# Last addition of every second tile of the final combination by GpSimd between its gathers

## What is computed

```python
topk_w, topk_idx = jax.lax.top_k(scores, K)                 # K = 2
cw = jnp.zeros((T, E), jnp.float32).at[jnp.arange(T)[:, None], topk_idx].add(topk_w)
y = jnp.einsum('te,teh->th', cw, expert_out).reshape(b, s, h)
y = y + _swiglu_mlp(x, sw_gate, sw_up, sw_down).reshape(b, s, h)
...
x = x + gb * y
```

## Time and profile before

| | us |
|---|---|
| median of 3 runs | 1524.89 (1524.53 to 1525.71) |
| the profiled execution, in all | 1526.7 |
| its span, first to last instruction | 1524.5 |
| TensorE busy in it | 1502.2 (99%) |
| VectorE busy | 983.0 (64%) |
| ScalarE busy | 729.5 (48%) |
| GpSimd busy | 713.5 (47%) |

### The profile page before, as it was taken

One profiled execution on the slowest core, in us unless ns is written; L12 is line 12 of the kernel. 1 busy time (PEld: TensorE's weight loads), 2 busy tenths in 40 slices (PEclk: granted clock), 3 DMA queues, 4 the chain that ended last, 5 costly groups with the idle time before them and its releaser, 6 DMA issues.

```text
span 1524.5 us, 29262 instructions
## 1 busy us (share of the span) xinstructions
PE 1502.2 (99%) x8812; PEld 1340.2 (88%) x8812; DVE 983.0 (64%) x2213; ACT 729.5 (48%) x1733; POOL 713.5 (47%) x767
## 2 busy tenths in 40 slices
PE   8999999999999999999999999999999999999997
PEld 4788888887999999999999999988999899999986
DVE  5977666677777777777777777785458322222258
ACT  4532222346666666666666666663332233333323
POOL 1113333446766665666565665769822211111054
PEclk9999999999999999999999999999999999999999
DMA  9336555577858486666757485746543555765576
GB/s 321 125 139 228 193 194 193 210 265 239 252 171 247 141 255 184 202 182 208 216 164 231 145 244 165 234 161 225 196 163 140 199 201 190 282 233 194 195 230 226
DMA packets 205600, 311.92 MB, mean 205 GB/s; under 512 B 80641, under 2 KB 142465, under 8 KB 198609
## 3 DMA queue, kind: packets, MB, share of 16 engines
q1 hardware_dynamic: 198400, 287.04, 56.6%
q0 software_dynamic: 5680, 18.62, 4.1%
q10 hardware_dynamic: 1440, 5.24, 0.9%
HBM read 189.97 MB, written 120.88 MB: 204 GB/s over the span
## 4 chain that ended last, share of the span: by engine, by line
PE 85%; DMA 4%; POOL 4%; DVE 3%; issue 2%; ACT 1%; SPq 1%; POOLq 0%; another core or an unknown queue 0%; ACTq 0%; DVEq 0%
PE bank L1624 45%; PE bank L1738 17%; PE bank L1853 7%; PE bank L1805 7%; PE bank L1836 4%; PE bank L1907 2%; PE bank L1941 1%; DMA h<-slot_results,pos_i 1%; DMA mod_early<-wmod 1%; POOL acc L1071 1%; POOL acc L1069 1%; DMA keys<-k_ring 1%; DMA ffn_rows<-h 1%; DMA w<-experts_lo 0%; DMA xr<-x 0%
## 5 line engine op out<-in xcount | busy, mean ns | idle before, releaser
L1624 PE MATMUL bank<-w,xt 128*128 (+2 forms) x1608 | 287.5, 327 | 0.3 <-ACT gate_s L1552 0.2
L1624 PEld LDWEIGHTS bank<-w,xt 128*128 128x128 f32 x1608 | 261.9, 188 | 6.6 <-DVE xt L2271 0.6
L1448 ACT ACTIVATE prob<-prob,row_inv 128x128 f32<-128x128 f32 (+3 forms) x256 | 137.3, 560 | 78.5 <-DVE row_inv L2308 78.3
L2427 DVE TENSOR_TENSOR ht_lo<-bank,ht_hi 128x128 fp32r<-128x128 f32 (+1 forms) x213 | 48.4, 282 | 181.0 <-ACT ht_hi L1567 176.4
L1436 ACT ACTIVATE prob<-bank,neg_max 128x128 f32<-128x128 f32 (+3 forms) x256 | 133.8, 526 | 42.3 <-DVE neg_max L2300 42.1
L1624 PE MATMUL bank<-wv_hi,h_hi 128*128 128x256 f32 x512 | 147.1, 287 | 0.0
L1624 PE MATMUL bank<-w,ht_hi 128*128 (+3 forms) x426 | 138.7, 406 | 6.8 <-DVE ht_lo L2427 5.9
L1624 PE MATMUL bank<-wv_hi,h_lo 128*128 128x256 f32 x512 | 144.7, 283 | 0.0
L1624 PE MATMUL bank<-wv_lo,h_hi 128*128 128x256 f32 x512 | 144.7, 283 | 0.0
L1248 POOL DMA_INDIRECT xin<-ffn_rows,slot_tokens x39 | 39.8, 1019 | 185.1 <-PE bank L1907 181.4
L2295 DVE TENSOR_REDUCE row_max<-bank 128x1 f32<-128x128 f32 (+3 forms) x256 | 119.7, 488 | 6.6
(11 more groups left out here) (252 smaller groups left out, 3882.7 us busy)
## 6 DMA issues: line engine op xcount, KB each, us to landing
keys<-k_ring SPq DMA_DIRECT2D x64, 512.0 KB, 3.2
ch_raw<-wexp SPq DMA_DIRECT2D x128, 170.0 KB, 3.2
experts_hi<-ch_hi SPq DMA_DIRECT2D x128, 170.0 KB, 2.6
experts_lo<-ch_lo SPq DMA_DIRECT2D x128, 170.0 KB, 2.8
w<-experts_hi SPq DMA_DIRECT2D x9, 2176.0 KB, 7.8
w<-experts_lo SPq DMA_DIRECT2D x9, 2176.0 KB, 14.5
q_transposed<-q_out SPq DMA_DIRECT2D x64, 256.0 KB, 2.1
k_even<-keys SPq DMA_DIRECT2D x16, 1024.0 KB, 5.7
```

The costliest lines, as they stand in the source:

```text
L1448: ins = act.activation(part, part, ACT.Copy, scale=row_inv[:, h, r:r + 1])
L1624: ins = pe.matmul(dst, a, m, start=(k == 0), stop=(k == last))
```

## The change

For the odd places below 12 (i = 1, 3, 5, 7, 9, 11, which are tiles 0 to 5) VectorE stops after the multiplication and raises `f_ok` there. The addition into `acc` is done by GpSimd, in `add_tile(i - 4)`, placed directly ahead of the gathers for place i = 5, 7, 9, 11, 13, 15. The new addition raises `h2_ok`, whose count stood at 16 (NT) until then, and both GpSimd's gathers for that place and SyncE's store of the tile wait for that count in place of `f_ok`.

```diff
         def finished(i):
 
+            if i % 2 and i < 2 * NB1:
+                return h2_ok, NT + (i + 1) // 2
             return f_ok, i + 1
...
+            def add_tile(i):
+
+                row = acc[:, GATHER[i], :]
+                pool.wait_ge(f_ok, i + 1)
+                pool.tensor_tensor(row, row, h2[:, i % TT, :], ALU.add).then_inc(h2_ok, 1)
+
             for i, t in enumerate(GATHER):
                 if i >= TT:
+                    if (i - TT) % 2:
+                        add_tile(i - TT)
                     pool.wait_ge(*finished(i - TT))
...
-                link(dve.tensor_tensor(a, a, mods[:, t // TT, 3, :], ALU.mult))
+                ins = dve.tensor_tensor(a, a, mods[:, t // TT, 3, :], ALU.mult)
+                if i % 2 and i < 2 * NB1:
+                    ins.then_inc(f_ok, 1)
+                    return
+                link(ins)
                 dve.tensor_tensor(acc[:, t, :], acc[:, t, :], a, ALU.add).then_inc(f_ok, 1)
```

## The result

The changed kernel takes 1535.2 us (median of 5 runs, 1532.0 to 1537.1), the kernel before 1525.2 us beside it (5 runs, 1524.5 to 1526.5). The ratio of the two is 1.006 with a 95% interval of 1.0049 to 1.0071: **slower by 9.2 us**, where 6.2 was forecast. The direction and the mechanism hold; the size is 3 us short. 1.006 of the 1524.89 from which the forecast started is 1534.0, near the top of its range (1534.8); the median itself, 1535.2, lies 0.4 us past it.

A forecast was written before the change was run, and what follows sets the result against it. GpSimd's own queue was taken to bound the tail: last gather 7.2 us later, less 0.95 for a quicker landing, makes +6.2 us on 1524.9, forecast 1531.1 us, range 1526.8 to 1534.8.

The forecast's parts named there:

- The bound and its end: In the last 66 us, the span's end moves as the last gather (place 15) moves, unless something else becomes later.
- The walk over GpSimd's list: GpSimd's steps summed from place 4 on: six odd places of 4.97 us, five even of 2.62; last gather 7.2 us later.
- The addition: Each of the six additions on GpSimd was taken at 1.29 us, from 22 earlier ones of the same shape.
- The gap: On GpSimd, from an addition's end to the gather waiting for it: 0.80 us, lower bound 0.15.
- Rival 1: GpSimd's queue runs ahead: gather 0.15 us behind the addition, only the last addition shows, 1525.3 us; chance 0.11.
- The hold-up of an addition by VectorE: VectorE operations with two SBUF inputs hold off each GpSimd addition in the tail by 0.3 us, bounds 0 to 0.6.
- The hold-up of gathers: Gathers xr behind an addition were taken at 1.25 us, between 1.01 when queued and 1.48 after a wait.
- The waits for `f_ok`: GpSimd's waits for VectorE before even places would already be met, for place 14 with some 4 us to spare.
- The landing: The last gather, with emptier DMA engines, lands in 4.5 us instead of 5.45, giving back 0.95 (bounds 0 and 2.05).
- From landing to end nothing is changed: The closing chain behind the last gather's landing, VectorE's work and the last store, stays at 10.3 us.
- rival 3: Late loads, or additions meeting two VectorE operations, make TensorE wait in the last job: another 3 us, 1534; chance 0.12.
- rival 2: GpSimd's 6.9 us of waits hide the additions and VectorE's saving comes through: 1.4 us faster, 1523.5; chance 0.05.

The follow-up runs named there:

- e_double: The changed kernel with a second GpSimd addition of the same size ahead of each of the six; 1541.99 us, ratio 1.0109 to the kernel before.
- e_noadd: The changed kernel without GpSimd's six additions, which VectorE does not do either; 1524.54 us, ratio 0.9997 to the kernel before.
- a_again: The changed kernel, unedited, profiled a second time; 1534.61 us, ratio 1.0058 to the kernel before.
- a_third: The changed kernel, unedited, profiled a third time; a single execution, 1536.06 us.
- e_tiny: The changed kernel with each of GpSimd's six additions over 4 of 512 columns only, all waits kept; 1527.67 us, ratio 1.0018 to the kernel before.
- e_hwait: The changed kernel with the wait for the addition moved from gather xr to gather h; 1530.64 us, ratio 1.003 to the kernel before.
- b_again: The kernel before, unedited, profiled a second time; 1524.83 us, ratio 0.9994.
- e_last: The changed kernel with only place 11's addition on GpSimd, VectorE doing the others as before; 1527.09 us, ratio 1.0008 to the kernel before.
- e_half: The changed kernel with only the additions of places 1, 5 and 9 on GpSimd, the others on VectorE; 1527.34 us, ratio 1.0015 to the kernel before.

## Why the prediction was right, and where it was short

**The bound and its end: right.** "The end moves as the last gather moves, unless something else becomes later still." e_double shows the first half (7.5 us in, 7.4 to 7.8 out by the medians), e_noadd that nothing else of the change matters, and the second half is what the sum then left out.

**The walk over GpSimd's list: right in sum, its terms partly by luck.** It put the last gather 1515.95 - 1467.10 = 48.85 us behind the mark; it stands at 48.4, 50.6 and 50.4. Term by term:
- The addition, 1.29 taken, is 1.30. The gap, 0.80 taken, is 0.79 to 0.80 in all six places of after, a_again, a_third, e_double and e_tiny. Rival 1, that the queue runs ahead (0.15), holds only where another gather stands between (e_hwait).
- The hold-up of an addition by VectorE, 0.3 each, 1.8 in all: none. The six additions take 1.29 to 1.31 in the three traces. An addition starts right behind a gather, 0.02 us after its end, and where the two meet it is VectorE that is held.
- The hold-up of gathers, taken as 0.24 for the six xr only, 1.4 in all: up to the last gather's start it is 2.7 us in the first trace of after and 4.8 in a_again, and gathers h and even places are long too. -1.8 + 1.3 gives 48.35 for the 48.4, -1.8 + 3.4 gives 50.45 for the 50.6. The total came close to the first trace because one term was too high and another too low: that is luck.
- The waits for `f_ok` are met from place 5 on, as forecast.

**The landing: right.** 4.5 us taken; 3.6 (1518.47 to 1522.11 in after), 4.8 and 4.2 measured.'s 3.3 was not reached. The Trainium skill's figure for such a DMA (DMA: Bandwidth & Descriptors, "Anatomy of one DMA"), 2.6 us by its formula, was reached nowhere; the rows decide.

**"From landing to end nothing is changed": wrong, 1.3 us.** From landing to end it was 10.3 us in both b_again and the first trace; it is 11.3, 11.6 and 11.9 in the three traces of after. VectorE's combination of place 13 stands ahead of `ht_lo` of the last job but one in VectorE's list. It now comes so late that TensorE, out of matrix work, stops for 3.1 us. What comes behind that is slower than before. Windows of the changed kernel (stretch, its length, busy time of PE, PEld, DVE, ACT and POOL, granted clock, DMA share, GB/s), then of b_again over the same matmuls:

```profile
1517.00:1519.00 2.00, 1.07 (x7) 0.78 (x5) 1.37 (x2) 2.00 (x6) 1.56 (x2) 1.00 0.83 300
1519.00:1521.00 2.00, 0.00 (x0) 0.00 (x0) 1.93 (x6) 0.01 (x1) 0.48 (x1) 1.00 0.72 181
1521.00:1523.00 2.00, 1.83 (x5) 1.46 (x6) 0.66 (x3) 0.72 (x1) 0.00 (x0) 0.68 0.54 211
1523.00:1525.00 2.00, 2.00 (x7) 1.49 (x6) 1.93 (x3) 0.00 (x0) 0.00 (x0) 0.50 0.00 0
```

```profile
1509.00:1511.00 2.00, 1.45 (x9) 1.16 (x8) 1.97 (x6) 0.90 (x3) 0.00 (x0) 1.00 0.76 253
1511.00:1513.00 2.00, 1.94 (x8) 1.61 (x9) 1.02 (x3) 0.72 (x1) 0.00 (x0) 1.00 0.37 138
```

TensorE is at 0.00 busy in 1519 to 1521, and then the granted clock is 0.68 and 0.50, the lower of its two levels, 1.2 of 2.4 GHz. The nine matmuls take 3.75 us; in b_again the same nine run from 1511.06 to 1513.41, 2.35 us. In a_again and a_third it is the last block, behind it, that ends the chain so: 3.93 and 4.22 us. Not every stop brings this: in the first trace of before TensorE waited 2.06 us for `ht_lo` ahead of its last block, and the clock stayed at 1.00 there; in e_last it fell after 1.91. A pair of them, in after and in b_again:

```profile
1522.16 1.05 PE L1634 MATMUL bank<-w,ht_hi 128*128 128x512 f32 x2
```

```profile
1511.87 0.62 PE L1624 MATMUL bank<-w,ht_hi 128*128 128x512 f32 x2
```

That is how TensorE comes back into a closing chain that the prediction had as VectorE's alone. The forecast's condition "unless something else becomes later still" named the loads as the candidate (rival 3), and these were not it: the last load of a turned tile is issued at 1502.01 in after, 3.2 us later than the walk had it, and no wait of TensorE for a load stands in the tail.

**The base: 1.25 us.** The sum was made against a trace whose tail was 57.4 us; undisturbed it is 56.15. The reference was one execution with a stop of VectorE just ahead of the mark, and its last gather came 0.7 to 1.0 us late. By the medians nothing showed this: they were 1524.9 and 1525.2, and the stop in the trace was hidden in a total that drifts by as much. Nor were GpSimd's 6.9 us of waits the reserve that rival 2 took them for: undisturbed it is 4.8 us, counted with the longer gathers. By the prediction's own walk the tail would have been 48.85 + 4.5 + 10.3 = 63.65 us long.

Together: 6.2 + 1.25 (base) + 0.95 (the walk, in the mean of three traces) - 0.3 (landing) + 1.3 (closing chain) = 9.4 us, against 9.5 from the traces. These terms are differences from the same traces and add up by themselves, but for rounding; the check from outside is the 9.2 of the medians.

**VectorE.** The prediction said that it would pay back part of what it saves at no cost, up to 1.2 us at one meeting. The first trace of after has two such meetings in its six additions, of 1.4 and 1.3 us, 2.7 together against the 4.3 saved. VectorE's timeline of after:

```profile
1476.73 2.16 DVE L2688 SCALAR_TENSOR_TENSOR h<-h,top_w,xr 128x512 f32<-128x512 f32 x1
...
1484.89 2.02 DVE L2703 TENSOR_TENSOR h<-h,mods 128x512 f32<-128x512 f32 x1
```

The first began 0.29 us ahead of the addition at 1477.02 and takes 2.16 us instead of 0.75; the second 2.02 instead of 0.69. In e_hwait all six are of this kind (2.01 to 2.24), and that kernel is the faster one, so they are not what made the changed kernel slow; that they cost nothing at all there was not tried. In e_last and e_half they reach TensorE, whose waits for `ht_lo` ahead of its last block there are 1.91 and up to 1.55 us. The Trainium skill says (SBUF — State Buffer, "SBUF: two separate sides") that VectorE with two SBUF inputs and GpSimd share a port with an exclusive lock, and that the one that starts first gets it, while the other one waits. The rows agree that one of the two stands still for about the other's length. They do not agree on which: in the row above VectorE's record begins 0.29 us first, and in e_hwait 0.14 to 0.38 us first, and yet it is VectorE that is held, while the addition takes its 1.3 us. The measurement decides. The 0.3 us that the forecast took for each held-up addition never appeared.

**What stays open.** Why the marks ahead of the tail lie between 1465.0 and 1470.1 with the same code; what stopped VectorE for 1.67 us in the first trace of before; why TensorE's clock fell after a stop of 1.91 us in e_last and not after 2.06 in the first trace of before; and what decides between the short and the long gathers, in after's traces and in e_tiny's. That it is the places at which GpSimd's and VectorE's lists meet is argued, and was not tried by a run in which VectorE's operations of two SBUF inputs are away.

## What to carry to other kernels

Work given to an engine "between" its DMA issues is only free if the engine is idle there and if nothing queued behind waits for the work: an instruction that the next one on its own engine waits for costs its time and, here, a gap of 0.79 us in place of 0.16, and one independent instruction put between them hides this. Before moving work off an engine, ask what a saving on that engine is worth (here 0.4 us, shown by leaving the work out), and count the tail from a mark inside it in two or three traces of the same kernel, since whole spans drift by several microseconds (the mark by 5 here, the change was 9). When the profile calls a gap "issue", compare it with the end of what the instruction waits for. When a chain is made later, look again at the engines that had ended level with it: they come back into the closing chain, here TensorE, at half of its clock after some 3 us without a matmul.

## What the runs showed of the hardware

- A gather that waits for GpSimd's instruction right ahead of it starts 0.79 us after that one's end, whether the instruction took 1.30 or 0.23 us; behind an instruction that it does not wait for it starts 0.15 to 0.16 us after.
- A gather of 128 rows takes 1.01 us of GpSimd at the least and up to 1.54 in the tail; that VectorE's work beside it makes the difference is argued.
- A gather whose wait for VectorE is met late starts 0.79 to 0.80 us after VectorE's instruction ends, also where the profile prints the gap as "issue" (b_again, 1501.13 to 1501.93).
- VectorE's instructions with two SBUF inputs take up to 2.4 us in place of 0.7 when they meet a GpSimd addition of 1.3 us (2.0 to 2.2 in e_hwait, 1.65 to 2.44 in e_half), and up to 3.69 where two additions follow one another (e_double). The addition itself is not held, though VectorE's record begins 0.14 to 0.38 us earlier (e_hwait).
- After 3.1 us without a matmul (after) TensorE's granted clock went to 0.50, and nine matmuls that take 2.35 us took 3.75, in other traces up to 4.22. It fell to 0.50 after a wait of 1.91 us in e_last too, and stayed at 1.00 after one of 2.06 in the first trace of before.
- Of 14 traces, one held a stop of 1.67 us on VectorE at the tail's beginning that no other showed; the profile gives no cause but "remote".
